# A four-layer conditional block on 16 batches: the second batch's generated rows kept in SBUF, late weight loads issued inside the turns, new orders of work, and unused products in TensorE's gaps of the start

## The chip, the core and the metric

The kernel runs on one core of a Trainium2 chip. A core has TensorE (the matmul array, with its weight loads), VectorE, ScalarE and GpSimd, which each run their own instructions in order, and SyncE, which here issues every DMA, all on one queue to 16 DMA engines. SBUF holds 128 partitions; PSUM has eight banks of 128 x 512 fp32. The metric is device time in microseconds, the median of several runs.

## The reference

All is fp32, with 16 batches of 256 rows of 256 columns.

```python
def L0(x, h, Wd, bd, Wu, bu, Wdd, bdd, Wdu, bdu):      # h: (16, 64)
    dWd = ((h @ Wdd.T + bdd) * 0.1).reshape(B, 128, 256)   # each batch has its own rows
    dWu = ((h @ Wdu.T + bdu) * 0.1).reshape(B, 256, 128)
    down = relu(einsum('bld,bnd->bln', x, Wd + dWd) + bd)
    return x + einsum('bln,bdn->bld', down, Wu + dWu) + bu

def L1(x, h, w, bias, lin_w, lin_b):                   # LayerNorm and a tanh gate
    out = layernorm(x) * w + bias + tanh(h @ lin_w.T + lin_b)[:, None, :]
    return out * w + bias

def L2(x, t, c, ...):                                  # adaLN block, 16 heads of 16
    g1, b1, g2, b2, a1, a2 = split(silu(silu(t @ W_t1.T + b_t1) @ W_t2.T + b_t2 + c) @ W_c.T + b_c, 6)
    q, k, v = split((layernorm(x) * g1 + b1) @ W_qkv.T + b_qkv, 3)
    x = x + a1 * (softmax(q k^T / 4) v @ W_o.T + b_o)
    h = gelu_tanh((layernorm(x) * g2 + b2) @ W_f1.T + b_f1) @ W_f2.T + b_f2
    return x + a2 * h

def L3(x, cond, norm_w, up_w, down_w):                 # RMSNorm, GEGLU, quantised down
    h = x * (cond @ norm_w.T + 1) * rsqrt(mean(x * x) + 1e-6)
    val, gate = split(h @ up_w.T, 2)
    return act_quant(val * gelu(gate)) @ weight_quant(down_w).T + x
```

`reference` applies L0 to L3 one after the other, with `cond_256` as condition.

## The kernel before

**Start.** The per-batch weights of L0 come from 16 chunks of 1 MB of `in_hyper`. TensorE multiplies each chunk (`generate`, L514) and ScalarE or VectorE copies the product, the rows of all 16 batches mixed over the partitions, into `gen` in SBUF. Two things leave `gen`: for the first batch eight rows of each chunk go straight into `cur` (`first_rows`, L366), and the whole of it is stored to `cur_scratch` in DRAM (L402), from which each later batch's `cur` is loaded (L391). In between small products make the gates and modulations. The weights `w_qkv`, `w_f1` and `w_up` come in raw (L399, L408, L410) and are split into a high part by ScalarE (L800) and a low part by VectorE (L1040); q, k, v, f and the up product are made as three fp32r products of such parts (`three`, L504). `wup_hi` lies where `gen` lay. All of these loads, `w_f2` and `w_down` (`late_weights`, L413, L414) are issued before turn 0's first own transfer.

**Turns.** Then come 19 turns. In turn t stage A works on batch t (L0, L1, first LayerNorm, q, k, v), B on batch t-1 (attention), C on t-2 (projection and feed-forward), D on t-3 (L3). The order in which each engine takes its steps is written by hand in three tables, `HEAD` (turns 0 to 5), `FULL` (one turn, repeated for 6 to 12) and `TAIL` (13 to 18), which `sequence` unrolls and each engine's `turn` carries out; an engine does its steps in that order and waits by semaphores.

The steps that matter here, by name and line: `A.down` (L572) and `A.up` (L578) are L0's products, ReLU between them on ScalarE (L822); `A.up` on VectorE adds the residual (L1106) and takes statistics; the LayerNorm's square roots are on GpSimd (`rstd`, L1301 to L1308); `A.ht` (L585) transposes; `A.q`, `A.k`, `A.v` are three times 12 products of 128x256 (L504); their biased results are split into `q_hi`, `k_hi` (ScalarE, L856) and `q_lo`, `k_lo` (VectorE, L1132), stored to `qk_scratch` (L420) and loaded again in another layout, head group by head group (`ql`, `kl`, L429), into `Qp` and `Kp`. `B.s0` to `B.s3` are scores (L634), each with two maxima on VectorE (L1140); `B.m0`, `B.m1` transpose the maxima (L640, `mt` L1154), which SyncE puts into `Qp` (L473); `B.t` are the second scores (L656) with exponentials (L870), `B.o` the products with V (L668); `C.proj` is L679, `C.f` L504, `C.g` L713, `C.xt` L722, `D.u` L504, `D.qt` L752, `D.y` L760. `A.cur` on VectorE (`combine`, L1056) makes the next batch's L0 weights, `cur * 0.1 + base`; it waits for `cur` to be loaded by SyncE's `A.load`:

```python
                if b == 0:
                    dve.wait_ge(first_in, 16 * NCH)
                else:
                    dve.wait_ge(cur_in, 16 * b)
```

`A.v` (`a_v`) waits for `qlo1`, the second part of `q_lo` of the same batch, because v's bank is q's; `A.k` waits in turn 1 for `klo1` of batch 0; `C.g0` waits for `klo1` of the batch in stage A.

## Time and profile before

| | us |
|---|---|
| median of 3 runs | 893.33 (892.43 to 893.88) |
| the profiled execution | 892.32 |
| its span | 890.5 |
| TensorE busy | 814.7 (91%) |
| VectorE busy | 551.0 (62%) |
| ScalarE busy | 520.9 (58%) |
| GpSimd busy | 235.1 (26%) |
| mean granted clock of TensorE | 0.946 of 2.4 GHz |

Times in the rows further down are in microseconds from the start of the span. The profile comes from one execution. A matmul's entry lasts until its result is out, so entries of a row of matmuls overlap; their spacing is what the engine needs. "Idle before" and the name behind it say how long an engine stood still before an instruction and what ended that. The idle time of an engine that nobody waits for costs nothing.

### The profile page before, as it was taken

What the parts mean: (1) busy time and instruction counts of PE and PEld (TensorE: products, weight loads), DVE (VectorE), ACT (ScalarE), POOL (GpSimd) and SP (SyncE); (2) the same over time, 40 slices, a digit from 0 to 9 for tenths busy, and PEclk for the clock granted to TensorE, in tenths of its full rate; (3) what the DMA queues carried; (4) which work ended last, traced back from release to release, by engine and by line L of the source; (5) the groups of instructions that cost most, each with busy time, mean ns of one, the idle gap of its engine ahead of it and who ended that gap; (6) DMA issues with size and microseconds to landing.
All of it is one profiled execution on the core that took longest, in us unless ns stands there. A gap on an engine that the chain in (4) does not pass through costs nothing.

```text
span 890.5 us, 15833 instructions
## 1 busy us (share of the span) xinstructions
PE 814.7 (91%) x5852; PEld 629.9 (71%) x5852; DVE 551.0 (62%) x1063; ACT 520.9 (58%) x808; POOL 235.1 (26%) x333
## 2 busy tenths in 40 slices
PE   6862477999999999999999999999999999999976
PEld 4212346777787878787878787878788787877665
DVE  1322567686767768585858585858585767656424
ACT  1112243566676758585867667666667676765642
POOL 1002213050505142423223140505050505030310
PEclk9855577999999999999999999999999999999999
DMA  9989733334242342424251514234242333230100
GB/s 346 382 309 409 234 130 112 117 113 150 71 163 72 110 135 85 160 85 161 84 162 52 178 64 151 94 117 129 102 139 102 119 114 107 102 101 3 31 13 12
DMA packets 56093, 118.48 MB, mean 133 GB/s; under 512 B 6000, under 2 KB 11504, under 8 KB 53312
## 3 DMA queue, kind: packets, MB, share of 16 engines
q1 hardware_dynamic: 56016, 117.48, 38.7%
q8 instruction: 46, 0.75, 0.3%
q14 instruction: 31, 0.25, 0.1%
HBM read 82.51 MB, written 34.16 MB: 131 GB/s over the span
## 4 chain that ended last, share of the span: by engine, by line
PE 80%; issue 8%; DVE 4%; DMA 3%; POOL 3%; ACT 1%; SPq 1%; POOLq 0%; DVEq 0%; ACTq 0%
PE bank L504 31%; PE bank L713 13%; PE pair_s L668 6%; PE pair_t L504 5%; PE bank L679 3%; PE bank L760 3%; PE pair_s L656 3%; PE pair_s L634 3%; DMA hyp<-in_hyper 2%; PE bank L572 2%; PE bank L578 2%; PE pair_t L656 2%; PE bank L752 2%; PE pair_t L634 1%; PE pair_t L514 1%
## 5 line engine op out<-in xcount | busy, mean ns | idle before, releaser
L713 PE MATMUL bank<-wf,G 128*128 128x256 f32 x512 | 126.6, 391 | 0.7 <-ACT G L885 0.5
L504 PE MATMUL bank<-wup_hi,hD_hi 128*128 128x512 f32 x256 | 110.2, 430 | 4.1 <-POOL hD_lo L1333 3.2
L1361 POOL TENSOR_TENSOR x<-x,xcr 128x512 f32<-128x512 f32 x16 | 20.8, 1301 | 335.4 <-DVE x L1198 335.4
L870 ACT ACTIVATE Pr<-pair_s 128x1024 f32<-128x1024 f32 x64 | 65.6, 1025 | 74.8 <-PE pair_s L656 74.8
L713 PEld LDWEIGHTS bank<-wf,G 128*128 128x128 f32 x512 | 92.2, 189 | 21.8 <-issue 5.8
L504 PE MATMUL bank<-wup_hi,hD_lo 128*128 128x512 f32 x256 | 101.6, 397 | 0.0
L504 PE MATMUL bank<-wup_lo,hD_hi 128*128 128x512 f32 x256 | 101.5, 396 | 0.0
L1140 DVE TENSOR_REDUCE nmax<-pair_s 128x4 f32<-128x1024 f32 x64 | 77.9, 1218 | 20.4 <-PE pair_s L634 20.3
L1164 DVE STREAM_TRANSPOSE oq<-pair_s 128x512 f32<-128x512 f32 x32 | 22.9, 717 | 88.7 <-PE pair_s L668 88.7
L1140 DVE TENSOR_REDUCE nmax<-pair_t 128x4 f32<-128x1024 f32 x64 | 77.4, 1210 | 0.0
L914 ACT ACTIVATE gl<-bank,rsD 128x512 f32<-128x512 f32 x64 | 43.8, 684 | 52.7 <-PE bank L504 52.5
L1208 DVE SCALAR_TENSOR_TENSOR hd<-bank,rsD,gl 128x512 f32<-128x512 f32 x64 | 47.8, 747 | 32.0 <-PE bank L504 30.8
L668 PE MATMUL pair_s<-Pr,Va 128*32 128x256 f32 x1024 | 65.1, 396 | 0.3 <-ACT Pr L870 0.2
L870 ACT ACTIVATE Pr<-pair_t 128x1024 f32<-128x1024 f32 x64 | 65.2, 1019 | 0.0
L504 PEld LDWEIGHTS bank<-wup_hi,hD_hi 128*128 128x128 f32 x256 | 48.3, 189 | 18.8 <-POOL hD_lo L1333 3.4
L504 PEld LDWEIGHTS bank<-wup_lo,hD_hi 128*128 128x128 f32 x256 | 48.4, 189 | 11.7
L504 PEld LDWEIGHTS bank<-wup_hi,hD_lo 128*128 128x128 f32 x256 | 48.6, 190 | 9.7
L668 PEld LDWEIGHTS pair_s<-Pr,Va 128*32 128x32 f32 x1024 | 29.6, 112 | 26.6 <-ACT Pr L870 8.4
L922 ACT ACTIVATE qT<-bank 128x1024 bf16<-128x1024 bf16 x32 | 32.8, 1024 | 23.6 <-PE bank L752 23.6
L504 PE MATMUL bank<-hA_hi,wqkv_hi 128*128 128x256 f32 x128 | 39.9, 312 | 3.4 <-POOL hA_lo L1333 3.4
L504 PE MATMUL bank<-hC_hi,wf_hi 128*128 128x256 f32 x128 | 38.1, 298 | 3.6 <-POOL hC_lo L1333 3.6
L1333 POOL TENSOR_TENSOR hA_lo<-hA,hA_hi 128x512 fp32r<-128x512 f32 x16 | 20.6, 1285 | 75.9 <-ACT hA_hi L849 75.9
(183 smaller groups left out, 2000.4 us busy)
## 6 DMA issues: line engine op xcount, KB each, us to landing
hyp<-in_hyper SPq DMA_DIRECT2D x16, 1024.0 KB, 8.6
Qp<-qk_scratch SPq DMA_DIRECT2D x64, 256.0 KB, 4.9
Kp<-qk_scratch SPq DMA_DIRECT2D x64, 256.0 KB, 4.7
qk_scratch<-q_hi SPq DMA_DIRECT2D x16, 512.0 KB, 2.8
qk_scratch<-k_hi SPq DMA_DIRECT2D x16, 512.0 KB, 3.4
tC<-rows_scratch SPq DMA_DIRECT2D x16, 384.0 KB, 4.3
xT_t<-in_xT SPq DMA_DIRECT2D x16, 256.0 KB, 4.3
x_t<-in_x SPq DMA_DIRECT2D x16, 256.0 KB, 4.5
```

Source lines behind the costliest of these rows:

```text
L504: mm = pe.matmul(dst, l, r, start=first and i == 0, stop=last and i == 2)
L634: mm = pe.matmul(pair[p % 2][:, half, r * L:(r + 1) * L], Qp[lo:lo + KR, 1 - par, p, r * P:(r + 1) * P], Kp[lo:lo + KR, 1 - par, p, :], st ...
L656: mm = pe.matmul(pair[p % 2][:, half, k * L:(k + 1) * L], Kp[lo:lo + KR, 1 - par, p, k * P:(k + 1) * P], Qp[lo:lo + KR, 1 - par, p, :], st ...
L668: mm = pe.matmul(bank[1][32 * j:32 * j + 32, (g % 2) * L:(g % 2 + 1) * L], Va[:, 1 - par, k, 4 * g + j, :], Pr[:, (2 * g + j // 2) % 4, j ...
L679: mm = pe.matmul(bank[5][:, r * D:(r + 1) * D], oT[:, k, r * P:(r + 1) * P], wo[:, k, :], start=k == 0, stop=k == KT - 1)
L713: mm = pe.matmul(bank[5][:, r * D:(r + 1) * D], G[:, k, r * P:(r + 1) * P], wf2[:, k, :], start=k == 0, stop=k == FT - 1)
L760: mm = pe.matmul(bank[6][:, 0:D], qT[:, k, :], wq3[:, k, :], start=k == 0, stop=k == FT - 1)
L870: act.activation(Pr[:, p % 4, :, :].rearrange("p a n -> p (a n)"), pair[p % 2][:, :, :].rearrange("p a n -> p (a n)"), ACT.Exp, scale=DH * ...
L914: act.activation(gl[:, n % 2, :], bank[6][:, :], ACT.Gelu, scale=rsD[:, 1, n // 2:n // 2 + 1]).then_inc(act_d, 1)
L922: act.activation(qT[:, :, :].rearrange("p k n -> p (k n)"), bank[7][:, :].bitcast(BF16), ACT.Copy).then_inc(act_d, 1)
L1140: dve.tensor_reduce(nmax[:, n % 2, :, p % GP, :], pair[p % 2][:, :, :].rearrange("p a (r n) -> p a r n", r=RT), AX.X, ALU.max, negate=True ...
L1208: dve.scalar_tensor_tensor(hd[:, (n % 2) * HALF:(n % 2 + 1) * HALF], bank[7][:, :], rsD[:, 1, n // 2:n // 2 + 1], gl[:, n % 2, :], ALU.mul ...
```

## The change

*The second batch.* A new tile `second` in the staging area takes eight more rows of every chunk, right behind the first batch's, with a semaphore `second_in`. `combine(1)` reads `second`, waits for `second_in` and for the up product of batch 0 (which reads `cur`), and no transfer of `cur` is made for batch 1; later batches wait for one `cur_in` less. `A.load` of turn 1 waits for `gen_out`, the store of `gen`.

*The transfers.* `w_qkv` is issued before the last four `first_rows`. The stores of `gen` and of the two constant planes, `w_f1`, `w_up` and the pair `w_f2`, `w_down` become steps `W.store`, `W.f`, `W.up` and `W.late` of SyncE's table: the first two at the head of turn 0, `W.up` in turn 0 among the head loads, `W.late` in turn 1 between the two `B.m`.

*The filler.* `keep_busy(n)` issues n products of 128x256 into bank 7 whose result nobody reads: one behind each of the chunks 6 to 14, six behind the last, 15 behind `A.up` of batch 0 and four behind its `A.ht`.

*The orders.* All three tables are new. What moves in the start is shown below. In the loop: `C.f3` comes before `A.ht`; `B.o0` before `D.qt1`; on VectorE `B.s3` before the second `A.ln`, and `B.m1` and `A.cur` before `A.k`; on GpSimd the next batch's `A.down` before `C.xt`; on SyncE `C.tc` and `D.y1` before most head loads. In turn 2 `A.lnb` follows `C.f1` on ScalarE. In the tail steps of C and D change places.

```diff
@@ load and store
                 sp.dma_start(cur[8 * c:8 * c + 8, :], gen[0:P:NB, c, :]).then_inc(first_in, 16)
+                sp.dma_start(second[8 * c:8 * c + 8, :], gen[1:P:NB, c, :]).then_inc(second_in, 16)
...
+                if b == 1:
+                    load_gates(b)
+                    return
                 sp.dma_start(cur[:, :], cur_rows[:, bass.ds(b, 1), :].rearrange("r o n -> (r o) n")).then_inc(cur_in, 16)
                 load_gates(b)
 
             load_rows(0)
+            sp.dma_start(wqkv_raw[:, :], w_qkv).then_inc(wqkv_in, 16)
             for c in range(NCH - 4, NCH):
                 first_rows(c)
             sp.wait_ge(rows_out, 16)
             load_gates(0)
-            sp.dma_start(wqkv_raw[:, :], w_qkv).then_inc(wqkv_in, 16)
...
-                        late_weights()
+                        {"store": store_rows, "f": f1_rows, "up": up_rows, "late": late_weights}[what]()
...
+                        if t == 1:
+                            sp.wait_ge(gen_out, 64)
@@ filler
+            def keep_busy(n):
+
+                for _ in range(n):
+                    pe.matmul(bank[7][:, 0:D], ident, wo[:, 0, :], start=True, stop=True)
+
             for c in range(6, NCH):
                 generate(c)
+                keep_busy(1 if c < NCH - 1 else 6)
...
+                    if a == 0:
+                        keep_busy(15)
...
+                    if a == 0:
+                        keep_busy(4)
@@ combine
                     dve.wait_ge(first_in, 16 * NCH)
+                elif b == 1:
+                    dve.wait_ge(second_in, 16 * NCH)
+                    dve.wait_ge(pe_a, at(PE_A, "up", 0))
                 else:
-                    dve.wait_ge(cur_in, 16 * b)
+                    dve.wait_ge(cur_in, 16 * (b - 1))
                 dve.wait_ge(dve_w, at(DVE_W, "base", 0))
-                dve.scalar_tensor_tensor(cur[:, :], cur[:, :], DELTA, base_c[:, :], ALU.mult, ALU.add).then_inc(cur_ready, 1)
+                dve.scalar_tensor_tensor(cur[:, :], second[:, :] if b == 1 else cur[:, :], DELTA, base_c[:, :], ALU.mult, ALU.add).then_inc(cur_ready, 1)
@@ HEAD of VectorE, turns 0 and 1
-        0: A.up A.lna A.lng A.ln W.qkv A.cur A.q 1: W.fa 0: A.k 1: A.up A.lna A.lng A.ln B.s0 B.s1 B.s2 B.s3 B.p0 B.m0 B.s4 B.s5 B.s6 B.s7 B.p1 B.m1
+        0: W.qkv A.cur A.up A.lna A.lng A.ln A.q A.k 1: A.up A.lna A.lng A.ln B.s0 B.s1 B.s2 B.s3 B.p0 B.m0 W.fa B.s4 B.s5 B.s6 B.s7 B.p1 B.m1 A.q
```

**VectorE in turn 0**, before: from the residual add of batch 0 (L1106) to k's low part (L1132); L1040 makes the low part of a weight, L1056 is the combine.

```order
L1106 TENSOR_TENSOR x<-bank,x_t 128x512
L1095 BN_STATS stA<-x 128x6 x2
L1099 BN_AGGR mvA<-stA 128x2 x2
L1114 SCALAR_TENSOR_TENSOR x<-x,mvA,w_t 128x256 x2
L1121 SCALAR_TENSOR_TENSOR x<-x,rsA,tA 128x256 x2
L1095 BN_STATS stA<-x 128x6 x2
L1099 BN_AGGR mvA<-stA 128x2 x2
L1040 TENSOR_TENSOR wqkv_lo<-wqkv_raw,wqkv_hi 128x1536
L1056 SCALAR_TENSOR_TENSOR cur<-cur,base_c 128x512
L1132 SCALAR_TENSOR_TENSOR q_lo<-bank,small,q_hi 128x256 x2
L1040 TENSOR_TENSOR wf_lo<-wf_raw,wf_hi 128x2048
L1132 SCALAR_TENSOR_TENSOR k_lo<-bank,small,k_hi 128x256 x2
```

And after, from the first batch's combine on:

```order
L1083 SCALAR_TENSOR_TENSOR cur<-cur,base_c 128x512
L1064 TENSOR_TENSOR wqkv_lo<-wqkv_raw,wqkv_hi 128x1536
L1083 SCALAR_TENSOR_TENSOR cur<-second,base_c 128x512
L1133 TENSOR_TENSOR x<-bank,x_t 128x512
L1122 BN_STATS stA<-x 128x6 x2
L1126 BN_AGGR mvA<-stA 128x2 x2
L1141 SCALAR_TENSOR_TENSOR x<-x,mvA,w_t 128x256 x2
L1148 SCALAR_TENSOR_TENSOR x<-x,rsA,tA 128x256 x2
L1122 BN_STATS stA<-x 128x6 x2
L1126 BN_AGGR mvA<-stA 128x2 x2
L1159 SCALAR_TENSOR_TENSOR q_lo<-bank,small,q_hi 128x256 x2
L1159 SCALAR_TENSOR_TENSOR k_lo<-bank,small,k_hi 128x256 x2
```

The low part of w_qkv and the second combine have moved from behind the LayerNorm to its front, the combine reads `second`, and w_f1's low part (`wf_lo`) has left this place for turn 1, where it stands behind the first `mt`.

**TensorE at the end of the start and in turn 0**, before: L514 are the chunks' products, L572 the down product of batch 0.

```order
L514 MATMUL pair_s<-hyp,condbd 32x512 x8
L514 MATMUL pair_t<-hyp,condbd 32x512 x8
L572 MATMUL bank<-xT_t,cur 128x256 x2
L578 MATMUL bank<-cur,dn 128x256 x2
L585 MATMUL bank<-small,x 128x128 x4
```

And after (L526 and L592 are the same lines; L571 is the filler):

```order
L571 MATMUL bank<-wo,small 128x256
L526 MATMUL pair_t<-hyp,condbd 32x512 x4
L571 MATMUL bank<-wo,small 128x256 x6
L592 MATMUL bank<-xT_t,cur 128x256 x2
L598 MATMUL bank<-cur,dn 128x256 x2
L571 MATMUL bank<-wo,small 128x256 x15
L607 MATMUL bank<-small,x 128x128 x4
L571 MATMUL bank<-wo,small 128x256 x4
```

A product of the filler stands behind each chunk, six ahead of the down product, 15 ahead of the transposes (L607) and four behind them. In turn 1, further on, all of `B.s0` to `B.s3` now stand ahead of `A.q` and `A.k`, and `B.m1` behind them as before.

**SyncE at the head loads of batch 0**, before: L413 and L414 are w_f2 and w_down, L391 the second batch's `cur`, L420 stores, L429 head loads.

```order
L410 DMA wup_raw<-in_w_up 128x4096
L413 DMA wf<-in_w_f 128x2048
L414 DMA wdn_raw<-in_w_down 128x2048
L391 DMA cur<-cur_scratch 128x512
L386 DMA tA<-rows_scratch 128x512
L379 DMA xT_t<-in_xT 128x512
L380 DMA x_t<-in_x 128x512
L420 DMA qk_scratch<-q_hi 128x2x512
L420 DMA qk_scratch<-q_lo 128x512
L420 DMA qk_scratch<-k_hi 256x1x512
L420 DMA qk_scratch<-k_lo 128x512
L429 DMA Qp<-qk_scratch 128x512
```

And after (L430 stores, L439 head loads, L420 w_up, L500 the gates of stage C):

```order
L430 DMA qk_scratch<-q_hi 128x2x512
L430 DMA qk_scratch<-q_lo 128x512
L430 DMA qk_scratch<-k_hi 256x1x512
L430 DMA qk_scratch<-k_lo 128x512
L439 DMA Qp<-qk_scratch 128x512 x2
L439 DMA Kp<-qk_scratch 128x512 x2
L439 DMA Qp<-qk_scratch 128x512
L439 DMA Kp<-qk_scratch 128x512
L420 DMA wup_raw<-in_w_up 128x4096
L439 DMA Kp<-qk_scratch 128x512
L439 DMA Qp<-qk_scratch 128x512
L500 DMA tC<-rows_scratch 128x768
```

Ahead of q's store there is now only w_f1 of the weights behind w_qkv; w_up has moved in front of the last two head loads, w_f2 and w_down behind this piece into turn 1, and `cur` for the second batch is gone.

## Rows read from the trace of the kernel before

**Rows 1.** Page, 40 slices of 22.3 us: granted clock in tenths, rate of transfers
```profile
PEclk9855577999999999999999999999999999999999
...
GB/s 346 382 309 409 234 130 112 117 113 150 71 163 72 110 135 85 160 85 161 84 162 52 178 64 151 94 117 129 102 139 102 119 114 107 102 101 3 31 13 12
```

**Rows 2.** Windows: busy us (instructions) of PE, PEld, DVE, ACT, POOL; clock, DMA, GB/s
```profile
300.00:800.00 500.00, 499.65 (x3796) 400.98 (x3796) 343.81 (x677) 342.35 (x531) 151.24 (x211) 1.00 0.36 116
```

**Rows 3.** TensorE's timeline: start, length, line, work, [idle before]
```profile
54.89 1.94 PE L514 MATMUL pair_t<-hyp,condbd 128*32 128x512 f32 x8 [0.71 <-DMA hyp<-in_hyper]
60.51 2.04 PE L572 MATMUL bank<-xT_t,cur 128*128 128x256 f32 x4 [3.68 <-DVE cur L1056]
...
74.38 1.12 PE L585 MATMUL bank<-small,x 128*128 128x128 f32 x4 [9.11 <-ACT x L832]
78.70 0.55 PE L504 MATMUL bank<-hA_hi,wqkv_hi 128*128 128x256 f32 x1 [3.20 <-POOL hA_lo L1333]
...
82.68 0.29 PE L504 MATMUL bank<-hA_hi,wqkv_hi 128*128 128x256 f32 x1
...
83.27 0.28 PE L504 MATMUL bank<-hA_lo,wqkv_hi 128*128 128x256 f32 x1
93.76 0.58 PE L504 MATMUL bank<-wqkv_hi,hA_hi 128*128 128x256 f32 x1 [10.21 <-DVE q_lo L1132]
...
97.47 2.05 PE L572 MATMUL bank<-xT_t,cur 128*128 128x256 f32 x4 [0.78 <-ACT Va L861]
...
121.15 0.50 PE L656 MATMUL pair_s<-Qp,Kp 64*128 64x256 f32 x4 [0.46 <-DVE mt L1154]
...
137.94 1.90 PE L679 MATMUL bank<-wo,oT 128*128 128x256 f32 x8
```

**Rows 4.** Timeline of VectorE, 50 to 200 us, same columns
```profile
70.10 1.97 DVE L1040 TENSOR_TENSOR wqkv_lo<-wqkv_raw,wqkv_hi 128x1536 fp32r<-128x1536 f32 x1
92.23 0.69 DVE L1056 SCALAR_TENSOR_TENSOR cur<-cur,base_c 128x512 f32<-128x512 f32 x1 [20.16 <-DMA cur<-cur_scratch]
...
93.62 2.28 DVE L1040 TENSOR_TENSOR wf_lo<-wf_raw,wf_hi 128x2048 fp32r<-128x2048 f32 x1
...
112.45 0.28 DVE L1154 CAST mt<-pair_s 32x128 fp32r<-32x128 f32 x1 [0.49 <-PE pair_s L640]
...
117.58 1.23 DVE L1140 TENSOR_REDUCE nmax<-pair_s 128x4 f32<-128x1024 f32 x1 [1.51 <-PE pair_s L634]
```

**Rows 5.** Timeline of GpSimd, 50 to 200 us
```profile
70.41 1.71 POOL L1301 TENSOR_TENSOR rsA<-mvA,eps_ln 128x2 f32<-128x2 f32 x1
...
107.28 0.20 POOL L1301 TENSOR_TENSOR rsA<-mvA,eps_ln 128x2 f32<-128x2 f32 x1
```

**Rows 6.** Timeline of ScalarE, 50 to 200 us
```profile
79.78 1.91 ACT L800 ACTIVATE wf_hi<-wf_raw 128x2048 fp32r<-128x2048 f32 x1 [2.56 <-DMA wf_raw<-in_w_f]
```

**Rows 7.** SyncE's timeline; DMA list: KB, median us to landing
```profile
77.56 0.34 SPq L391 DMA_DIRECT2D cur<-cur_scratch  x1
...
Qp<-qk_scratch SPq DMA_DIRECT2D x64, 256.0 KB, 4.9
...
cur<-cur_scratch SPq DMA_DIRECT2D x15, 256.0 KB, 2.8
wup_raw<-in_w_up SPq DMA_DIRECT2D x1, 2048.0 KB, 10.0
```

**Rows 8.** Windows, columns as in rows 2
```profile
57.00:59.00 2.00, 0.00 (x0) 0.00 (x0) 1.18 (x2) 0.00 (x0) 1.16 (x1) 0.50 0.05 15
70.00:74.00 4.00, 0.00 (x0) 0.00 (x0) 2.07 (x2) 0.76 (x2) 3.12 (x5) 0.50 1.05 409
```

**Rows 9.** Timelines of TensorE and VectorE in one turn of the loop
```profile
537.14 0.27 PE L640 MATMUL pair_s<-small,parts 128*32 128x128 f32 x1
...
539.43 1.99 PE L713 MATMUL bank<-wf,G 128*128 128x256 f32 x8
...
537.24 0.88 DVE L1132 SCALAR_TENSOR_TENSOR k_lo<-bank,small,k_hi 128x256 fp32r<-128x256 f32 x2 [0.84 <-ACT k_hi L856]
```

More of the change, by code:

```diff
@@ L72 @@
     "SP": """
[L73 to L76 removed]
+        0: W.store0 W.f0 A.load A.qs A.ks A.ql0 A.ql1 A.kl0 A.kl1 A.ql2 A.kl2 W.up A.kl3 A.ql3 2: C.tc 1: A.load B.m0 W.late B.m1 A.qs A.ks A.ql0
@@ L101 @@
+        A.up C.ht A.lna A.ln A.ht C.g3 6: A.down 5: C.xt 6: C.proj C.ln A.up C.ht A.lna A.ln""",
 }
@@ L279, in cond_seq_kernel @@
         s2 = staged("s2", [P, KT, NB], F32, KT * NB)
+        second = staged("second", [P, 2 * D], F32, 2 * D)
         assert stage_at <= nc.sbuf_base, (stage_at, nc.sbuf_base)
@@ L398, in _, with store_rows, f1_rows, up_rows @@
             load_gates(0)
[L399 to L410 removed]
+            def store_rows():
+                for i in range(4):
+                    sp.dma_start(cur_scratch[4 * i:4 * i + 4].rearrange("c p n -> p c n"), gen[:, 4 * i:4 * i + 4, :]).then_inc(gen_out, 16)
+                sp.wait_ge(zero, 6)
+                sp.dma_start(qk_scratch[0, :, 3, :], ys[:, :, :].rearrange("p r n -> p (r n)")).then_inc(planes_out, 16)
+                sp.dma_start(qk_scratch[1, :, 3, :], Kp[:, 1, 0:2, :].rearrange("p c n -> p (c n)").bitcast(F32)).then_inc(planes_out, 16)
+            def f1_rows():
+                sp.dma_start(wf1_raw[:, :], w_f1).then_inc(wf1_in, 16)
+            def up_rows():
+                sp.wait_ge(gen_out, 64)
+                sp.dma_start(wup_raw[:, :], w_up).then_inc(wup_in, 16)
             def late_weights():
```

121 lines of the change are left out of this document (57 added, 64 removed).

## The prediction

> **What bounds the kernel now.** I read the page's slices first, then TensorE's timeline of the first 180 us, then the timelines of the engines that it waits for. The slices, 22 us each, show a start in which the DMA engines move 309 to 409 GB/s and TensorE's granted clock is mostly 0.5, which is 1.2 GHz, and behind it a clock of 1.0, 2.4 GHz [rows 1]. From 300 to 800 us TensorE is busy for 499.65 of 500 us, VectorE for 343.81 [rows 2]. These are the turns of the loop; no order of the same products can shorten them, it can only bring waits in. Time can be won in the start, and what is won there reaches the end whole, because every later turn waits for TensorE alone.
>
> In the start, TensorE's timeline shows the first batch's down product at 60.51 us, its q products at 78.70, the last k product at 83.27, and then nothing for 10.21 us until v at 93.76, named as a wait for q_lo on VectorE [rows 3]. VectorE had been free for 20.16 us: the combine of the second batch's rows stands ahead of q_lo in its order and waits for a DMA that SyncE issued at 77.56, behind the rows' store and five large weight loads [rows 4, 7]. So the likeliest item to fall is this wait, and the question is what is late next.
>
> **The change, part by part.** The sum follows the start of the first batch's projection in turn 2, 137.94 now [rows 3]; behind that point TensorE is nearly always busy.
>
> Start of the first batch. 16 more small copies and w_qkv (768 KB) now stand in the queue ahead of the last rows. From 57 to 59 us, just ahead of the first batch, the DMA engines moved only 15 GB/s [rows 8], so the queue was empty. That hides about what w_qkv adds (0.79 MB at the 346 to 409 GB/s of the busy slices [rows 1] is some 2.1 us). The small copies add 256 KB, 0.7 us, all but the last of it in front of the last big chunk. I take +0.5 us; bounds -0.9 (the last chunk's products, 1.94 us at the low clock [rows 3], run at the high one) and +1.5.
>
> VectorE in turn 0. The combine goes ahead of the residual add and waits for the up product as that does: +0.69 us, the length of one combine [rows 4]. The low part of w_qkv, 1.97 us, leaves the place where it now runs beside the LayerNorm of GpSimd. There GpSimd's add took 1.71 us against 0.20 for the same one in turn 1 [rows 5], and its end is on the path: -1.5 us. In its new place VectorE waits for products anyway, if the weights are there by then.
>
> The wait itself. q_lo no longer stands behind a transfer, so v follows k: -10.2 us. TensorE then is in a run of products. Its clock rose at 82.68, where the products' spacing went from 3.98 us for 18 to 0.59 for 5 [rows 3], and the 12 products of v take 1.4 us instead of 2.6: -1.2. ScalarE now makes w_f1's high part (1.91 us [rows 6]) between v and the ReLU of turn 1, against a down product of 1.03 us when fast: and behind a slow down product (2.04 [rows 3]) it comes now: the ReLU is some 0.3 earlier than now relative to v, and the up product saves 1.1 if the clock holds: -1.4 together, bounds -1.4 and +0.9.
>
> The filler. 128x256 fp32 products like these take 0.24 us each at the high clock (eight in 1.90) and 0.5 at the low one (four in 2.04 [rows 3]). One behind each chunk, 0.24 or 0.5, fits the 0.71 us that TensorE waits for the next one [rows 3]; six before the first batch need 1.4 to 3.1 of the 3.6 us there, 15 behind the up product 3.6 to 7.5 of some 9, four behind the transposes 1 to 2 of 3.2 [rows 3]. They cost nothing on the path. What do they give? After the 15 TensorE stands still again for 2 to 5 us until the transposes. In the trace an idle stretch of 3.20 us came ahead of q, and q began at 1.2 GHz [rows 3]. So I expect the high clock in parts only: -1.0 us of the down, up, q and k products; bounds 0 and -4.3 (2.0 of down and up, 0.5 of the transposes, 1.8 of the 18 slow products, all at twice the speed).
>
> Turn 1. VectorE's w_f1 low part, 2.28 us [rows 4], moves into the row of maxima, behind mt. The maxima there already wait 1.51 us because one pair of scores stands behind q on TensorE [rows 4], and that wait goes as all scores now precede q: net nothing there. But the m1 transposes now follow q and k, 24 products, which can only start behind the last scores. From mt to the second pass of the scores (112.45 to 121.15) is 8.7 us now. After: 2.5 us for mt and w_f1, two maxima of 1.2, a pair of scores 0.8, the 24 products 2.8 at the high clock or 5.2 at the low one, 1.0 for m1 and mt: 9.4 to 11.8. TensorE has little to do before it, so I take 11.2: +2.5, bounds +0.7 and +3.1. The 4.4 us of w_up's low part stay behind the first exponentials, as now; |w_down|'s sum moves ahead of o1's evacuation into an idle stretch: 0. From the second scores to the projection is 16.8 us now [rows 3]; with one of the two slow A*V groups fast, -0.5 (bounds 0 and -1.7).
>
> Turn 2 and later. The second LayerNorm of batch 2 now waits behind one GELU more and the transposes wait for it: +0.5. In the loop, POOL's, SP's and ScalarE's moves have slack of a microsecond or more. The tightest is VectorE: k_lo now stands behind mt and the combine, and the first f2 products wait for it. m1 ends at 537.41 [rows 9]; with 0.3, 0.7 [rows 4] and 0.88 us [rows 9] behind it, k_lo ends near 539.3, and the f2 product starts at 539.43 [rows 9]. Covered by 0.1 us: 0, bound +1.2 for 0.1 in each of twelve turns. Head and tail orders otherwise: 0, bounds -1.0 and +1.5; I add +0.5 for these two.
>
> **Sum:** +0.5 +0.7 -1.5 -10.2 -1.2 -1.4 -1.0 +2.5 -0.5 +0.5 +0.5 = -11.1 us. The profiled execution took 892.3, 1.8 above its span of 890.5, and 1.0 under the median of 893.3. So the span should come to 879.4, and the time to 882.2.
>
> A transfer in the turns can undo part. In the trace the row that sat behind weights landed only in time for a combine at 92.23, 14.7 us after its issue, where 2.8 is the median [rows 4, 7]. Now w_up (2 MB, 10.0 us to landing [rows 7]) is issued ahead of the last two head loads. By the sum k's low part is done near 83.5; its store and the five issues behind it take some 5, an estimate, so the two go at 88.5 and land, 10.0 and 4.9 us later [rows 7], near 103.4. The last scores want them near 102.0 (mt, 112.45 less 14.1, then 2.5 and one maximum).
> The Trainium skill, "DMA: Bandwidth & Descriptors", section "Queues, rings and completion order", says that each DMA engine takes a queue's descriptors in ring order; by that rule the heads do wait for all of w_up, and the last scores come 1.4 us late. The wait at 92.23 agrees.
>
> **Rivals.**
> *Weights in the way.* As just worked out: +1.4 in turn 1, and w_f2 and w_down (2 MB) do the same to the small Qp rows of the second half, which have some 5 us to spare. 883.6. For it: everything goes through one queue. Against it: the 10.0 us hold with other traffic, and six loads may be through sooner.
> *The filler keeps the clock.* If TensorE is at 2.4 GHz from the first batch on, -4.3 instead of -1.0, and -1.7 more in turn 1: 882.2 - 5.0 = 877.2. Against it: the idle stretches that it leaves.
> *The wait moves on.* The second batch's x and xT are behind 5.8 MB of stores and w_f1. At the 409 GB/s at which the trace moves them [rows 8] all is there about 16 us after 60, near 77, and turn 1 wants it near 84.5 (97.47 [rows 3] less 13). If the transfers took 5 to 10 us longer than that cover, or the second batch's copies were that late, half or all of the 10.2 us would be back: 887 to 892.
> *Slower.* If the f2 products wait in each turn of the loop for k_lo on VectorE: k_lo moved by 1.2 us against now (mt 0.3, combine 0.7, a start after m1 0.2). Were there no slack, twelve turns would lose 14.4 us: 896.6. It decides from 0.9 us per turn on (11.1 in twelve). Against it: the cover of 0.1 us above, and a VectorE that is busy for 69% of the loop's time [rows 2].
>
> **How the numbers follow.** The forecast 0.62, weights in the way 0.14, filler 0.13, wait moves on 0.07, slower 0.04. Without the last two, the high end is that of the open terms together, +1.0 for the start, +1.0 for the filler, +2.3 for the ReLU and up, +0.6 for turn 1: 887. The low end is that of -1.4 for the start, -3.3 for the filler and -1.8 for turn 1: 875.7, rounded to 876. About 0.2% (1.8 us) is what a measurement of this kernel can tell from none. Faster takes the first three and most of the fourth, 0.94; same 0.02; slower 0.04.
>
> **What would show it.** v directly behind k, with no wait for q_lo (right) or a wait of TensorE ahead of the second batch's down product for x (the wait moved on). The first q product near 78 and its spacing, 0.22 or 0.12 us (filler). GpSimd's eps add at 0.2 us. The last scores of turn 1 released by a maximum or by a DMA. k's products between them and m1. The projection of turn 2 near 126.3 to 127. The idle time of TensorE between 300 and 800 us, 0.35 us now. I am wrong if the projection comes before 122 or after 131, or if the loop's turns grow.

## The result, and the profile of the changed kernel

| | before | changed |
|---|---|---|
| median of 9 runs each, us | 892.33 (888.13 to 893.88) | 887.38 (884.85 to 889.79) |
| ratio | | 0.9951, 95% interval 0.9936 to 0.9966 |
| profiled execution, its span, us | 892.3, 890.5 | 886.4, 884.6 |

The change wins 4.4 us (0.49%) by the ratio; 882.2 had been forecast, with 887 as the upper end of the range. The profiled executions differ by 5.9 us, 1.0 more than the medians; those of the changed kernel spread over 5 us.

First TensorE's timeline of the changed kernel, which answers to [rows 3] (start, length, line, work, number of records, [idle before and who ended it]).

```profile
57.25 1.07 PE L526 MATMUL pair_t<-hyp,condbd 128*32 128x512 f32 x8 [1.32 <-DMA hyp<-in_hyper]
58.25 2.86 PE L571 MATMUL bank<-wo,small 128*128 128x256 f32 x12
64.52 1.83 PE L592 MATMUL bank<-xT_t,cur 128*128 128x256 f32 x4 [3.41 <-DVE cur L1083]
...
68.78 8.02 PE L571 MATMUL bank<-wo,small 128*128 128x256 f32 x30
77.24 0.66 PE L607 MATMUL bank<-small,x 128*128 128x128 f32 x4 [0.44 <-ACT x L856]
...
81.10 0.36 PE L516 MATMUL bank<-hA_hi,wqkv_hi 128*128 128x256 f32 x1 [1.48 <-POOL hA_lo L1360]
...
84.60 0.39 PE L516 MATMUL bank<-wqkv_hi,hA_hi 128*128 128x256 f32 x1 [0.43 <-DVE q_lo L1159]
...
87.06 1.10 PE L592 MATMUL bank<-xT_t,cur 128*128 128x256 f32 x4 [0.78 <-ACT Va L885]
...
93.56 0.80 PE L658 MATMUL pair_s<-Kp,Qp 64*128 64x256 f32 x4 [3.29 <-DMA Kp<-qk_scratch]
...
111.09 0.51 PE L680 MATMUL pair_s<-Qp,Kp 64*128 64x256 f32 x4 [0.46 <-DVE mt L1181]
...
126.77 1.89 PE L703 MATMUL bank<-wo,oT 128*128 128x256 f32 x8
```

The wait of 10.21 us for `q_lo` is gone: v follows k after 0.43 us. But the last chunk's products start 2.36 us later than they did, and the first down product 4.01 us later; 0.5 had been forecast for that. Who held it is in VectorE's and GpSimd's timelines, which answer to [rows 4, 5]:

```profile
63.68 0.69 DVE L1083 SCALAR_TENSOR_TENSOR cur<-cur,base_c 128x512 f32<-128x512 f32 x1 [4.00 <-DMA cur<-gen]
...
69.08 0.69 DVE L1083 SCALAR_TENSOR_TENSOR cur<-second,base_c 128x512 f32<-128x512 f32 x1 [3.04 <-issue]
...
83.67 0.88 DVE L1159 SCALAR_TENSOR_TENSOR q_lo<-bank,small,q_hi 128x256 fp32r<-128x256 f32 x2 [9.12 <-ACT q_hi L880]
```
```profile
74.79 0.19 POOL L1328 TENSOR_TENSOR rsA<-mvA,eps_ln 128x2 f32<-128x2 f32 x1
```

The first batch's combine waited 4.00 us for the last copy of eight rows. The second batch's combine now runs at 69.08 behind no transfer; `q_lo` waits for ScalarE only; GpSimd's add takes 0.19 us instead of 1.71.

The accounts of the two profiled executions, by the start of the product named:

| from, to | before | changed | difference | forecast |
|---|---|---|---|---|
| start, first down product | 60.51 | 64.52 | +4.01 | +0.5 |
| to the first transposes (`A.ht`) | 13.87 | 12.72 | -1.15 | -0.8 |
| to q | 4.32 | 3.86 | -0.46 | filler |
| to v | 15.06 | 3.50 | -11.56 | -10.2 and filler |
| to the second down product | 3.71 | 2.46 | -1.25 | -1.2 |
| to the second pass of the scores | 23.68 | 24.03 | +0.35 | -1.4 +2.5 |
| to the first projection | 16.79 | 15.68 | -1.11 | -0.5 |
| to the down product of turn 6 | 183.36 | 184.36 | +1.00 | +0.5, and a share of +0.5 |
| to that of turn 15 | 420.35 | 420.24 | -0.11 | 0 |
| to the last transposes of turn 17 (`C.xt`) | 121.61 | 124.69 | +3.08 | the rest of +0.5 |
| to the end | 27.24 | 28.54 | +1.30 | 0 |

From the first down product to the projection the items come to -15.2, where -12.6 had been forecast, so the projection stands at 126.77, where 126.3 to 127 had been expected, in spite of the later start: two misses, +3.5 and -2.6, hide each other there. Against the forecast of -11.1 the whole lacks 5.2: +3.5 in front of the first batch, -2.6 up to the projection, +0.4 up to turn 15, and +3.9 behind it, of which 1.3 are in the last turn. The loop did not grow: nine turns take 420.24 us instead of 420.35. TensorE's idle time between 300 and 800 us is 1.40 us instead of 0.35, and 1.26 of that are three waits in turns 15 and 16.

The tail's loss shows in part as small waits. TensorE's timeline of the changed kernel from turn 15 on, six of the lines that carry a wait (there are eight between 780 and 830, 3.65 us together, where the kernel before had three in the same stretch: 0.46, 0.37 and 1.48 us):

```profile
791.89 0.38 PE L516 MATMUL bank<-hC_hi,wf_hi 128*128 128x256 f32 x1 [0.34 <-POOL hC_lo L1360]
...
796.99 0.50 PE L658 MATMUL pair_s<-Kp,Qp 64*128 64x256 f32 x4 [0.46 <-DVE mt L1181]
...
805.24 0.50 PE L680 MATMUL pair_s<-Qp,Kp 64*128 64x256 f32 x4 [0.46 <-DVE mt L1181]
...
808.82 0.50 PE L680 MATMUL pair_t<-Qp,Kp 64*128 64x256 f32 x4 [0.42 <-ACT Pr L894]
...
814.05 0.50 PE L680 MATMUL pair_s<-Qp,Kp 64*128 64x256 f32 x4 [0.38 <-DVE oq L1191]
...
824.02 1.99 PE L703 MATMUL bank<-wo,oT 128*128 128x256 f32 x8 [1.14 <-DVE oT L1203]
```

Longer waits are only half of the loss. From the down product of turn 15 to the transposes of turn 17 TensorE is busy for 118.52 of 124.69 us, before for 116.98 of 121.61, with 835 matmul records and a granted clock of 1.00 in both. Idle and busy time each grew by 1.54. That fits products which, split up by more waits, overlap less, but no run isolates it.

### The profile page after: what moved, and what is told of

Its sections match the earlier page's. It is cut to its first block, busy times and chain, and to the rows that moved or that the text cites. A ratio compares the mean times of both kernels' runs of the same rounds, so it can differ in the third digit from the quotient of the medians.

```text
span 884.6 us, 15989 instructions
## 1 busy us (share of the span) xinstructions
PE 823.8 (93%) x5920; PEld 638.4 (72%) x5920; DVE 552.4 (62%) x1063; ACT 526.8 (60%) x812; POOL 232.5 (26%) x333
## 4 chain that ended last, share of the span: by engine, by line
PE 80%; issue 7%; DMA 5%; DVE 3%; POOL 2%; ACT 2%; SPq 1%; POOLq 0%; DVEq 0%; ACTq 0%
PE bank L516 31%; PE bank L737 13%; PE pair_s L692 6%; PE pair_t L516 5%; PE bank L703 3%; PE bank L784 3%; PE pair_s L680 3%; PE pair_s L658 3%; DMA hyp<-in_hyper 2%; PE bank L776 2%; PE pair_t L680 2%; PE pair_t L658 2%; PE bank L592 1%; PE bank L598 1%; DMA x_t<-in_x 1%
## 5 line engine op out<-in xcount | busy, mean ns | idle before, releaser
L692 PEld LDWEIGHTS pair_s<-Pr,Va 128*32 128x32 f32 x1024 | 29.1, 111 | 28.1 <-ACT Pr L894 7.9
L856 ACT ACTIVATE xc<-xc,rsC 128x256 f32<-128x256 f32 x32 | 17.5, 595 | 41.2 <-POOL rsC L1335 41.2
```

Of the source, the lines that this page charges most:

```text
L692: mm = pe.matmul(bank[1][32 * j:32 * j + 32, (g % 2) * L:(g % 2 + 1) * L], Va[:, 1 - par, k, 4 * g + j, :], Pr[:, (2 * g + j // 2) % 4, j ...
```

## Experiments

All are timed in five rounds beside the kernel before; ratios are to that, with 95% intervals. The changed kernel stands at 0.9951 by the same measure. The intervals of E1 to E4, E6 and E7 overlap its own, so what these say of a stage rests on the traces, one execution each, and on how well a stage repeats from kernel to kernel.

**E1. Without the unused products.** They are 34 in all.
```diff
-                keep_busy(1 if c < NCH - 1 else 6)
-                    if a == 0:
-                        keep_busy(15)
-                    if a == 0:
-                        keep_busy(4)
```


> The changed kernel without the 35 unused products (one behind each of nine chunks, six and fifteen and four before q). Nothing else is touched. My theory: they are what made the q, k, v and turn-1 products run at the high clock, and cost nothing on the path. In the trace of after, q's products are 0.12 us apart and down and up of the first batch run at 1.2 GHz in any case. Without them q and k should come 2.9 us later (24 products at 0.22 instead of 0.12, and the four transposes), so the projection at 129 to 131 instead of 126.77, and the time 889.5 to 891.5 instead of 887.4. Rival: the filler itself delays the chunks (its products stand ahead of the next chunk's on TensorE); then the last chunk starts nearer to 54.9 than to 57.25 and the time stays within 1 us of after.

889.24 us, 0.9971 (0.9956 to 0.9985). The start of q in TensorE's timeline:

```profile
82.28 0.55 PE L516 MATMUL bank<-hA_hi,wqkv_hi 128*128 128x256 f32 x1 [3.20 <-POOL hA_lo L1355]
82.63 0.41 PE L516 MATMUL bank<-hA_hi,wqkv_lo 128*128 128x256 f32 x1
82.85 0.41 PE L516 MATMUL bank<-hA_lo,wqkv_hi 128*128 128x256 f32 x1
```

0.21 us from one to the next instead of 0.12; the second down product comes at 89.84 instead of 87.06 and the projection at 129.22 instead of 126.77. The last chunk starts at 57.57 without them, so they do not delay the chunks. The unused products are worth 2.5 us in the trace, 1.8 by the ratios, whose intervals just overlap.

**E2. w_qkv back behind the first batch's rows.**
```diff
-            sp.dma_start(wqkv_raw[:, :], w_qkv)...        # behind load_rows(0)
+            sp.dma_start(wqkv_raw[:, :], w_qkv)...        # behind load_gates(0)
-  ACT 0: W.qkv A.down ...     DVE 0: W.qkv A.cur A.up A.lna A.lng A.ln ...
+  ACT 0: A.down W.qkv ...     DVE 0: A.cur A.up A.lna A.lng A.ln W.qkv ...
```


> The changed kernel with w_qkv's load back behind the first batch's last rows and its gate load, and the two low/high part steps back behind the first batch's residual and LayerNorm on VectorE and behind the down product's evacuation on ScalarE. Theory: w_qkv's 0.79 MB, some 2 us, stood ahead of the last row copies, and is 1.6 of the 4.0 us by which the first down product came late; with it gone down starts at 62.9 (still 2.4 late by the copies), but GpSimd's add comes beside the low part again (+1.5), so the projection stays within 0.5 of 126.8 and the time within 0.5 of after. Rival: the queue was empty anyway, and w_qkv costs nothing: down stays at 64.5 and the time rises by 1.5.

886.60 us, 0.9949 (0.9931 to 0.9967). TensorE, then GpSimd:

```profile
57.10 1.06 PE L526 MATMUL pair_t<-hyp,condbd 128*32 128x512 f32 x8 [1.27 <-DMA hyp<-in_hyper]
...
62.42 1.10 PE L592 MATMUL bank<-xT_t,cur 128*128 128x256 f32 x4 [1.47 <-DVE cur L1083]
```
```profile
71.10 1.71 POOL L1328 TENSOR_TENSOR rsA<-mvA,eps_ln 128x2 f32<-128x2 f32 x1
```

From the last chunk to down it takes 5.32 us instead of 7.27: w_qkv ahead of the last row copies cost 2.0. GpSimd's add takes 1.71 us again, beside the low part of w_qkv, but the down and up products of the first batch now run at the high clock (1.10 and 1.13 us instead of 1.83 and 2.08), and the second down product is at 85.34, still 1.7 earlier than in the changed kernel. The projection is at 126.94, as expected, but not for the expected reason: turn 1 took 41.60 us instead of 39.71, and that stretch differs from trace to trace (see E10).

**E3. The second batch's copies behind the first batch's.**
```diff
-                sp.dma_start(second[8 * c:8 * c + 8, :], gen[1:P:NB, c, :]).then_inc(second_in, 16)
+            for g in range(8):     # behind load_gates(0)
+                sp.dma_start(second[g:P:8, :], gen[1 + NB * g:2 + NB * g, :, :]).then_inc(second_in, 16)
```


> The changed kernel with the second batch's rows fetched by eight copies of 32 KB behind the first batch's last copy, instead of sixteen of 16 KB, one behind each chunk's. Theory: each small copy takes 0.2 to 0.4 us of the queue though it moves only 16 KB, and the twelve that fall before the last chunk make its products start at 57.25 instead of 54.89. Then the last chunk here starts at 54.9 to 55.3, down at 62.2 to 62.6, the projection at 124.5 to 125.2, and the time is 1.5 to 2.3 us under that of after, 885.3. Rival: the copies cost what their bytes cost (0.04 us each); then the last chunk stays near 57.0 and the time is that of after.

884.78 us, 0.9921 (0.9901 to 0.9941). TensorE's timeline:

```profile
54.12 1.06 PE L527 MATMUL pair_t<-hyp,condbd 128*32 128x512 f32 x8 [0.87 <-DMA hyp<-in_hyper]
...
60.41 1.39 PE L593 MATMUL bank<-xT_t,cur 128*128 128x256 f32 x4 [2.44 <-DVE cur L1084]
...
64.24 8.46 PE L572 MATMUL bank<-wo,small 128*128 128x256 f32 x30
72.70 0.66 PE L608 MATMUL bank<-small,x 128*128 128x128 f32 x4
```

The last chunk starts at 54.12, 3.13 us earlier, the projection at 123.09. The other traces agree: the last chunk starts between 57.03 and 57.57 in the six kernels with the changed kernel's copies (it, E1, E2, E4, E6, E7) and between 53.72 and 54.39 in the five without (E3, E8, E9, E10, E12). In E3 it is also 0.8 us ahead of the 54.89 of the kernel before, for a reason that no run shows, so 3.1 us is the upper figure for the copies; E5 below gives 1.8. The windows of 44 to 52 us (busy us of the five, clock, DMA share, GB/s), of before, the changed kernel and E3, show how: the DMA engines are busy throughout in all three, and move 408, 358 and 395 GB/s. In the same window the other kernels with the copies move 357 to 379, those without 396 to 401.

```profile
44.00:52.00 8.00, 5.80 (x24) 0.60 (x24) 1.14 (x2) 0.92 (x2) 0.00 (x0) 0.50 1.02 408
```
```profile
44.00:52.00 8.00, 4.24 (x28) 1.07 (x28) 0.69 (x1) 0.60 (x1) 0.00 (x0) 1.00 1.01 358
```
```profile
44.00:52.00 8.00, 4.98 (x34) 1.36 (x30) 1.39 (x2) 0.60 (x1) 0.00 (x0) 1.00 1.01 395
```

The fifteen products behind `A.up` now end only at 72.70 and the transposes start without a wait; their data were ready at 72.64 (ScalarE). That cover is used up.

**E11. The copies twice.** A third copy of 16 KB behind each chunk's two, into a buffer that nothing reads.
```diff
+                sp.dma_start(third[8 * c:8 * c + 8, :], gen[2:P:NB, c, :]).then_inc(third_in, 16)
```


> The changed kernel with a third copy of 16 KB behind each chunk's two, of the third batch's rows into a buffer that nothing reads. Theory: what the copies cost is per copy, 0.2 to 0.25 us of the queue each; twelve more put the last chunk's products from 57.25 to 59.6 and the time from 887.4 to 889.8. Rival: bytes, or a cost that comes once with the first: last chunk at 57.25 to 57.8, time within 0.7 us of after.

893.38 us, 1.0023 (1.0005 to 1.0042).

```profile
61.33 1.07 PE L528 MATMUL pair_t<-hyp,condbd 128*32 128x512 f32 x8 [1.36 <-DMA hyp<-in_hyper]
```

The last chunk is 4.08 us later, where 59.6 had been expected for it, and the whole change's gain is gone. Eleven of the added copies are issued ahead of that chunk's load, which makes 0.37 us each; the other comparisons give 0.16 (E5 below: 56.64 against 54.89) and 0.28 us (E3). By bytes it would be 0.04. These are averages, not a fixed price: over the last four steps the chunks come 2.64 us apart before, 3.06 in the changed kernel and 3.02 here, with twice the copies. SyncE's own time is not what delays them: it issued the last chunk's load at 46.13 in the changed kernel and at 46.31 in the one before.
The Trainium skill, "DMA: Bandwidth & Descriptors", section "Why a DMA increments its semaphore by 16 and not by 1", says that a DMA goes to the largest number of engines, up to 16, that divides the slowest dimension of both its access patterns; by that rule a copy of eight rows goes to eight of the 16 engines. A copy would then add 2 KB to the 64 KB that each of these moves per chunk, 3% or 0.08 us of 2.6, an estimate by that page's rule and a fifth to a half of what is measured. No run here shows on how many engines a copy ran, nor where the rest comes from.

**E5. The direct rows alone.** The kernel before with the buffer `second`, its copies and the combine from it (`combine(1)` reads `second`, SyncE loads only the gates for batch 1); every order, every weight load as before, no unused products.

> The kernel before with one thing changed: the second batch's rows are copied straight into a buffer of their own as the change does it, so the combine on VectorE waits for no late transfer. Order of the weights' loads, orders of the engines and all else as before, no unused products. Theory: the wait of 10.2 us for q_lo goes, but in the kernel before the second batch's x and xT are also behind the row store and the weights in SyncE's queue (GpSimd waited for x until 94.65), so TensorE's next wait is for xT ahead of the second down product, near 93 to 94 instead of 97.47; with the copies' +2.4 at the start the projection comes 2 to 4 us earlier than 137.94 and the time is 888 to 890. Rival: all of the 10.2 us goes by this alone and the moved loads give nothing; then the second down product is at 89 to 90, the projection near 131, and the time 885 to 886.

891.13 us, 0.9998 (0.9984 to 1.0013), above the 888 to 890 expected; the trace is 3.0 us shorter than before's, and the medians do not show that: the profiled execution was the fastest of its twelve.

```profile
56.64 1.93 PE L519 MATMUL pair_t<-hyp,condbd 128*32 128x512 f32 x8 [0.97 <-DMA hyp<-in_hyper]
...
95.23 2.07 PE L577 MATMUL bank<-xT_t,cur 128*128 128x256 f32 x4 [7.38 <-DMA xT_t<-in_xT]
```

The wait moved on, as the third rival of the prediction had it for this case: the second down product waits 7.38 us for `xT`, behind the rows' store and the weights in SyncE's queue. With the dearer start (the last chunk at 56.64 instead of 54.89), nothing that the medians can tell is left. So it takes both halves of the change, the rows' direct way and the weights' transfers moved into the turns: without the second, 7.38 of the 10.2 us stay.

**E4. The orders of turns 13 to 18 of before.** The five entries of `TAIL` as before, fitted to the new seams of `FULL`; for instance TensorE's turn 16:
```diff
-  16: B.s0 C.proj D.u0 B.s1 D.u1 C.ht D.u2 C.f0 C.f1 C.f2 B.m0 B.s2 D.u3 B.s3 D.qt0 C.f3 D.y0 B.m1 B.t0 C.g0 ...
+  16: C.proj B.s0 D.u0 D.u1 C.ht B.s1 D.u2 C.f0 C.f1 C.f2 B.m0 C.f3 B.s2 D.u3 B.s3 C.g0 D.qt0 C.g1 B.m1 B.t0 ...
```


> The changed kernel with the five engines' orders from turn 13 to 18 put back to those of before (the seams to the loop as the change has them). Theory: in the traces the time from the down product of turn 15 to the end was 148.9 us before and 153.2 after, and the new orders of turns 15 and 16 are the cause of 2 to 4 us of it: 883.4 to 885.4 against 887.4. Rival: the difference lies in the granted clock, which fell to 1.2 GHz in the last turn in the one trace and not in the other, and is not a matter of the orders: the time stays within 0.7 us of after.

885.70 us, 0.9932 (0.9912 to 0.9953).

```profile
855.48 0.66 PE L745 MATMUL bank<-small,x 128*128 128x128 f32 x4 [1.25 <-POOL x L1387]
...
875.75 1.50 PE L783 MATMUL bank<-wq,qT 128*128 128x256 bf16 x8 [1.12 <-ACT qT L945]
...
879.32 1.89 PE L783 MATMUL bank<-wq,qT 128*128 128x256 bf16 x8 [1.12 <-ACT qT L945]
```

From the down product of turn 15 (733.85) to these transposes it takes 121.63 us: before's 121.61, not the changed kernel's 124.69. All 3.1 us are the orders' doing: this stretch takes 121.56 to 121.63 us in all seven kernels with the old tail and 124.60 to 124.69 in all seven with the new one. From there to the end it takes 28.5 as in the changed kernel: the last 1.3 us are something else. By the medians the gain is 1.7 us; in its profiled execution the projection happened to come 2.4 us later, at 129.21, by slower products in turn 1 (see E10).

**E7. The orders of turns 2 to 5 of before.** As E4, for `HEAD` from turn 2 on.

> The changed kernel with the five engines' orders of turns 2 to 5 put back to those of before (the sum of |w_down| stays in turn 1, seams to turn 1 and to the loop as the change has them). Theory: from the projection of turn 2 to the down product of turn 6 it is 183.36 us in the trace of before and 184.30 to 184.36 in those of after and its variants, so the new orders there cost 1.0 us, and the time is 0.6 to 1.3 under after's. Rival: the 1.0 us comes from the transfers of w_up, w_f2 and w_down that the change moves into these turns, not from the orders; then the time is that of after.

887.17 us, 0.9942 (0.9926 to 0.9959). From the projection (129.29) to the down product of turn 6, in TensorE's timeline, 183.33 us:

```profile
312.62 1.03 PE L592 MATMUL bank<-xT_t,cur 128*128 128x256 f32 x4
```

That is before's 183.36 and not the changed kernel's 184.36, with the weights' transfers where the change puts them: the orders cost 1.0 us. In all other traces too the stretch is longer with the new orders (183.99 to 184.36) than with the old (182.56 to 183.36). The ratios, 0.9942 against 0.9951, are too close to show it.

**E6. Unused products in the last turn.**
```diff
+                    if c == NB - 1:
+                        keep_last(12)          # behind the last transposes of C.xt
+                    if d == NB - 1:
+                        keep_last(4)           # behind D.qt
```


> The changed kernel with more unused products, in the last turn: twelve behind the last transposes of the second block's output (TensorE waits 3.15 us there for hD_lo) and four behind each of the two transposes of quantized rows (it waits 1.12 us there for qT). Theory: the products behind those waits run at 1.2 GHz in the trace of after (the first eight up products 0.43 us apart instead of 0.23, the last eight of y in 1.89 instead of 1.05, the last transposes in 1.04 instead of 0.62); with the gaps filled they run at 2.4 and the end comes 2 to 2.9 us earlier: 884.5 to 885.4. Rival: the clock in the last turn does not follow such short gaps, or the fillers stand in the way of work that comes back early: within 0.7 us of after.

887.11 us, 0.9943 (0.9927 to 0.9960): no gain. TensorE's last turn, and the same products in the changed kernel:

```profile
858.63 5.34 PE L576 MATMUL bank<-wo,small 128*128 128x256 f32 x24
863.63 0.58 PE L516 MATMUL bank<-wup_hi,hD_hi 128*128 128x512 f32 x1
...
882.37 1.04 PE L793 MATMUL bank<-wq,qT 128*128 128x256 bf16 x8
```
```profile
876.42 1.27 PE L784 MATMUL bank<-wq,qT 128*128 128x256 bf16 x8 [1.12 <-ACT qT L946]
...
880.00 1.89 PE L784 MATMUL bank<-wq,qT 128*128 128x256 bf16 x8 [1.12 <-ACT qT L946]
```

The clock did follow: the last eight products of y take 1.04 us instead of 1.89. The surer sign is the first eight up products behind the gap of 3.15 us: they take 1.97 to 2.05 us in the five kernels with products in that gap, 3.02 to 3.58 in the nine without. But twelve unused products show 24 records and take 5.34 us of a gap of 3.15. Each fp32 product is two records, 0.44 us together at the high clock; I had priced a product at one record here and in the prediction. The up products started 1.7 us late and ate the gain: from the transposes to the end it takes 28.1 us instead of 28.5.

**E8. Together.** E3, E4 and E6, and w_qkv's load directly behind the first batch's last row copy, with its high part on ScalarE behind `A.down`.

> The changed kernel with the copies for the second batch behind the first batch's (eight of 32 KB), the orders of turns 13 to 18 of before, the unused products in the last turn, and w_qkv's load directly behind the first batch's last row copy, in front of the gate row. If the terms measured so far add up (2.4 at the start by the copies, 3.1 in turns 15 to 17 by the orders, 1.0 for w_qkv out of the way of the last rows, 2 for the clock in the last turn) it takes 878.5 to 880.5. If the clock's term is nil, 881 to 882. If w_qkv is still in the way (first down product later than 59.8), 1 us more.

880.96 us, 0.9875 (0.9854 to 0.9896), just above the 878.5 to 880.5 expected. The first down product is at 58.92. But on VectorE the second batch's combine now waits for its copies, and the first batch's residual add waits behind it:

```profile
65.17 0.69 DVE L1092 SCALAR_TENSOR_TENSOR cur<-second,base_c 128x512 f32<-128x512 f32 x1 [0.86 <-DMA second<-gen]
65.78 0.68 DVE L1142 TENSOR_TENSOR x<-bank,x_t 128x512 f32<-128x512 f32 x1
```

**E9. Refined.**
```diff
-  DVE 0: W.qkv A.cur A.up A.lna A.lng A.ln ...
+  DVE 0: W.qkv A.up A.lna A.lng A.ln A.cur ...
-  keep_last(12) ... keep_last(4)          and HEAD from turn 2 as in E7
+  keep_last(5) ... keep_last(2)
```


> The one before (all together) with three things more: the combine of the second batch on VectorE behind the first batch's LayerNorm instead of ahead of its residual add (there it waited for the copies until 65.17, and the residual add with it, 3 us behind the up product); the orders of turns 2 to 5 of before; five unused products instead of twelve behind the last transposes (twelve took 5.34 us of a gap of 3.15) and two instead of four behind the quantized rows' transposes. If the terms add up: residual add at 64.3 (-1.5), -1.0 from projection to turn 6, last turn -1.7: 876.5 to 877.5 against 880.96. Rival: the orders of turns 2 to 5 gave 1.0 in the trace but only 0.2 in the median, and the last turn's products fall back to 1.2 GHz: 879 to 880.

879.01 us, 0.9856 (0.9832 to 0.9880). That is the rival's 879 to 880, but not by its cause. From the transposes of turn 17 to the end it takes 25.8 us instead of 28.5, as expected, and the orders of turns 2 to 5 give 0.7. The transposes of the first batch are at 71.75 instead of 73.32, but the next line gives that back: the second down product waits 3.02 us for `xT` and comes at 83.80 (83.43 in E8), and the projection at 126.18 (124.22).

```profile
83.80 1.35 PE L597 MATMUL bank<-xT_t,cur 128*128 128x256 f32 x4 [3.02 <-DMA xT_t<-in_xT]
```

**E10. Unused products in turn 1.**
```diff
+                    if a == 1:
+                        keep_busy(5)                    # behind A.up
+                    if b == 0:
+                        keep_busy((2, 3, 3, 0)[n])      # behind B.s(n); 1 behind B.t(0), B.t(2), B.o(0)
```


> The kernel just above with unused products in the gaps of turn 1 too: five behind the second up product, two, three and three behind the pairs of the first scores, one behind each of the first and third pairs of the second scores and behind the first row of products of A and V. Theory: the granted clock fell to 0.5 in 90 to 105 us in all traces, and q's and k's products of turn 1 and the slow row of A*V cost 2 to 3 us by it; with the gaps filled it stays 1.0 and from the second down product to the projection it takes 38.5 to 39 us instead of 40.6; time 1.8 to 2.3 us under that kernel. Rival: in that stretch VectorE's maxima set the pace, or the fillers hold back the scores that come back early: no gain, or 1 us lost.

875.11 us, 0.9815 (0.9790 to 0.9841). The windows of turn 1, of the changed kernel and of E10:

```profile
95.00:105.00 10.00, 4.66 (x25) 3.34 (x25) 9.44 (x11) 4.63 (x6) 2.87 (x6) 0.50 0.97 364
105.00:121.00 16.00, 11.27 (x99) 8.36 (x101) 14.19 (x17) 9.93 (x13) 1.28 (x1) 0.82 0.66 260
```
```profile
95.00:105.00 10.00, 7.20 (x50) 5.50 (x50) 9.51 (x11) 5.55 (x5) 1.41 (x1) 1.00 0.99 362
105.00:121.00 16.00, 12.52 (x127) 7.83 (x126) 12.80 (x17) 9.42 (x13) 1.28 (x1) 1.00 0.69 266
```

The granted clock was 0.50 and 0.82 and is 1.00. Between 91 and 95 us, behind a wait of 2.58 us for `Kp`, it still fell, to 0.60. From the second down product to the projection it takes 37.34 us; in the changed kernel it took 39.71, in E1 39.38, in E2 to E4 and E6 to E9 between 40.56 and 42.38, with the clock near 0.5 before the second scores in each, and again behind them in a part that differs. Behind the second scores the gain is clear: from there to the projection it takes 13.93 us here and 13.90 in E12, which has the same products, against 15.62 to 17.01 in all twelve others. Ahead of them it is not: 23.41 here, 25.50 in E12, 23.68 to 25.65 in the others. By the medians the gain is 3.9 us where 1.8 to 2.3 had been expected; E9, from which it is counted, has the slowest turn 1 of all traces. E10's own runs still spread over 4.9 us, from a cause that no trace here shows.
The Trainium skill, "TensorE: Matmul & The Clock Gate", Part 1, says that "the default state is throttled, and activity releases the throttle". By that rule products that nobody reads keep up the clock of the work behind a gap; the rows above agree (0.50 and 0.82 without them, 1.00 with them).

**E12. w_f1 behind the first heads.**
```diff
-  SP 0: W.store0 W.f0 A.load A.qs A.ks A.ql0 A.ql1 A.kl0 A.kl1 A.ql2 ...   ACT 0: ... A.v W.fa 1: A.down A.lnb
+  SP 0: W.store0 A.load A.qs A.ks A.ql0 A.ql1 A.kl0 A.kl1 W.f0 A.ql2 ...   ACT 0: ... A.v 1: A.down W.fa A.lnb
```


> The kernel just above with w_f1's load behind the loads of the first four head pieces instead of ahead of the second batch's x and xT, and its high part on ScalarE behind the second down product's evacuation. Theory: in turn 1 the second down product waits 1.44 to 3.02 us for xT and the first scores 2.58 to 4.25 us for Kp, both behind w_f1's 1 MB in the queue; with it behind them the first scores start 2 to 2.5 us earlier (88.5 instead of 90.8) and the time is 1.5 to 2.5 us under 875.1. Rival: the store of the rows (4 MB) and the stores of the q and k planes set when the heads arrive, or the low part of w_f1, now later, holds VectorE's second maxima: no gain, or up to 1 us lost.

874.67 us, 0.9824 (0.9790 to 0.9857): the same as E10.

```profile
89.19 0.50 PE L665 MATMUL pair_s<-Kp,Qp 64*128 64x256 f32 x4 [1.93 <-DMA Kp<-qk_scratch]
...
101.98 0.50 PE L665 MATMUL pair_s<-Kp,Qp 64*128 64x256 f32 x4 [1.85 <-DMA Qp<-qk_scratch]
```
```profile
96.30 2.29 DVE L1081 TENSOR_TENSOR wf_lo<-wf_raw,wf_hi 128x2048 fp32r<-128x2048 f32 x1 [0.73 <-ACT wf_hi L841]
```

The first scores start at 89.19 instead of 90.80, and the second down product no longer waits for `xT`. But w_f1's low part now waits for its high part, at 96.30, and the last scores wait 1.85 us for `Qp` behind w_up; the second pass of the scores comes at 107.80 instead of 106.65. The wait moved on again, and the 1.5 to 2.5 us expected did not come.

## Why the prediction was wrong

**Start of the first batch: +0.5, bounds -0.9 and +1.5, measured +4.0.** Both terms were mis-sized, and of the 4.0 us 2.36 lie ahead of the last chunk and 1.65 behind it. The copies were priced by their bytes, 0.7 us in all, and held to stand nearly all in front of the last chunk (eleven of the sixteen do); the traces show 1.8 to 3.1 for them (E5, E3), E11 still more for each further one. w_qkv was held to fit into the stretch of 57 to 59 us in which the queue was empty [rows 8]. But the last row copy is issued behind the last chunk's product, at 59.10, and what stands ahead of it in the queue must go first: E2 shows 2.0 us. The empty stretch was real, but a load that fills it holds up the row copy that is issued in it. The late chunks made that worse and are not all of it: in E3, with no copies ahead, it takes 6.29 us from the last chunk to the first down product, against 4.92 to 5.08 in the four kernels that have w_qkv behind the rows as well. The bounds came from the same two prices and so shared their fault.

**Head and tail orders otherwise: 0, bounds -1.0 and +1.5, measured +1.0 and +3.1.** I compared only the loop's tightest place and took the rest to be as good as before. E7 and E4 show that the new orders cost four microseconds, more than the bound of 1.5: in the tail eight small waits where there had been three, and as much again in longer busy time. Which moved step makes which wait no run separates. No row of before shows that; the difference of the two orders in turns 15 to 17 might have, had each moved step been followed to its releaser. The range left this term out as well: its high end of 887 adds up the other open terms at their bounds. With this one's +1.5 in place of the +0.5 that was counted it would have been 888, above the measured 887.38.

**The last turn, +1.3, was not in the sum.** TensorE stands still there for 3.15 us and again for 1.12 before its last products, and whether these run at 1.2 or 2.4 GHz differs from trace to trace (eight products of y in 1.05 us in before, E5 and E7, in 1.50 and 1.89 in E4, which has before's orders there). In E9, with products in the gaps, they take 1.05 again. What decides it where the gaps stay open is not shown.

**The wait itself, -10.2: right**, and v behind k as forecast. The rival by which the wait moves on was no danger to the whole change, and was the whole truth for half of it (E5). The weights in the way: in the changed kernel the last scores were released by a maximum; only where the start came earlier (E3, E8, E10, E12; not in E9) did a transfer hold them, 2.15, 1.93, 1.12 and 1.85 us.

**The filler, -1.0, bounds 0 and -4.3: 1.8 to 2.5** (E1), inside the bounds; the price of one product was wrong by half (0.44 us, two records). The fifteen took 8.02 us, and the gap held them with 0.44 us to spare, which was luck at that price.

**ReLU and up of turn 1, mt to t0: +1.1 forecast, +0.35 measured; t0 to the projection -0.5, -1.1.** About right: `mt` comes at 100.57, so the first term is -1.5 where -1.4 was forecast and the second +1.8 where it was +2.5, all inside their bounds. E10 and E12 show that the stretch behind t0 hung on the clock; for the one ahead of it they do not.

**k_lo in the loop: 0, right**, the slower case did not come. The projection came between 122 and 131, the mark that I had set for being wrong; but that mark watched only the start, where two misses hid each other, and 3.9 of the 5.2 us that are lacking lay behind turn 15. The 126.3 to 127 named for it is not what the sum gives either: its items up to there make 125.8, since two of the +0.5 lie behind the projection.
